# Weight quantization inside an attention and feed-forward kernel: half-width tiles with four load and two store buffers

## The reference

```python
def _weight_quant(w):
    scale = 1.0 / jnp.clip(jnp.mean(jnp.abs(w)), 1e-05)
    wq = jnp.clip(jnp.round(w * scale), -1.0, 1.0) / scale
    return w + jax.lax.stop_gradient(wq - w)

gate = jax.nn.silu(_bitlinear(x, w_gate))
up = _bitlinear(x, w_up)
return _bitlinear(gate * up, w_down)
```

## Time and profile before

| what | value |
|---|---|
| median of 11 runs | 3708.01 us (3695.86 to 3712.17) |
| profiled execution, its own time | 3701.79 us |
| span of its slowest core (core 1) | 3700.2 us |
| spans of the 8 cores | 3681.3 to 3700.2 us |
| TensorE (matmul), VectorE, ScalarE busy | 47%, 37%, 30% of the span |
| mean granted clock of the cores | 0.635 to 0.709 |

### The profile page before, as it was taken

One profiled execution on the slowest core, in us unless ns is written; L12 is line 12 of the kernel. 1 busy time (PEld: TensorE's weight loads), 2 busy tenths in 40 slices (PEclk: granted clock), 3 DMA queues, 4 the chain that ended last, 5 costly groups with the idle time before them and its releaser, 6 DMA issues.

```text
span 3700.2 us, 31906 instructions; the slowest of 8 cores (3681.3 to 3700.2 us)
## 1 busy us (share of the span) xinstructions
PE 1753.8 (47%) x8824; PEld 593.5 (16%) x8824; DVE 1354.7 (37%) x2709; ACT 1114.6 (30%) x1276; POOL 18.8 (1%) x55
## 2 busy tenths in 40 slices
PE   1211112222004443447477577728755862962874
PEld 0000000000001110111111111103322321421331
DVE  1442454444225554432321311134524524443352
ACT  1322322221120001547478488811201211220120
POOL 1000000000000000000000000000000000000000
PEclk9999998555555555555555555558987995986998
DMA  5445354222330000010100100023223322422522
GB/s 119 148 159 170 136 209 115 74 68 59 117 128 14 12 0 12 1 46 1 46 1 1 46 1 1 1 98 112 76 80 123 97 77 91 139 60 69 165 61 77
DMA packets 140978, 278.36 MB, mean 75 GB/s; under 512 B 7944, under 2 KB 106504, under 8 KB 134664
## 3 DMA queue, kind: packets, MB, share of 16 engines
q1 hardware_dynamic: 107256, 192.96, 15.8%
q10 hardware_dynamic: 24320, 67.12, 5.4%
q0 software_dynamic: 9232, 16.25, 2.8%
HBM read 250.61 MB, written 41.94 MB: 79 GB/s over the span
## 4 chain that ended last, share of the span: by engine, by line
PE 20%; ACT 15%; DVE 11%; DMA 7%; issue 5%; DVEq 1%; ACTq 0%; SPq 0%
PE ps_f L1076 6%; PE ps_f L1082 6%; PE ps_f L1190 5%; DMA wdbuf<-scr_d 4%; ACT PTb L747 4%; ACT PTb L743 4%; ACT PT L743 3%; ACT PT L747 3%; DMA xo_t<-xo 2%; ACT hqT L30 2%; DVE den_sb L821 1%; PE ps_sc L719 1%; DMA x1f<-scr_x 1%; PE ps_den L774 1%; DMA wubuf<-scr_u 1%
## 5 line engine op out<-in xcount | busy, mean ns | idle before, releaser
L719 PE MATMUL ps_sc<-qn,khat 32*128 32x512 bf16 (+3 forms) x1280 | 312.0, 529 | 136.8 <-ACT PT L743 50.1
L1190 PE MATMUL ps_f<-wdbuf,hqT 128*128 128x512 bf16 x1024 | 265.9, 410 | 99.8 <-DMA wdbuf<-scr_d 48.8
L1076 PE MATMUL ps_f<-wgbuf,xqT 128*128 128x512 bf16 x1024 | 248.3, 386 | 113.8 <-DMA wubuf<-scr_u 112.9
L1082 PE MATMUL ps_f<-wubuf,xqT 128*128 128x512 bf16 x1024 | 242.8, 380 | 0.0
L755 DVE TENSOR_TENSOR PT<-PT,maskD 128x512 bf16<-128x512 bf16 x64 | 27.2, 425 | 487.5 <-ACT PT L747 487.5
L323 ACT ACTIVATE wfbuf<-wfbuf,magicc,sclw 128x1024 f32<-128x1024 f32 (+1 forms) x48 | 100.5, 2093 | 322.9 <-DMA wfbuf<-wdT 173.1
L743 ACT ACTIVATE PT<-ps_sc,negMb 128x1024 bf16<-128x1024 f32 (+3 forms) x160 | 157.8, 986 | 121.3 <-PE ps_sc L719 109.1
L366 PE MATMUL ps_tr<-ident,xst 128*128 128x128 bf16 x384 | 52.2, 304 | 299.2 <-DVE xTc L29 207.4
L1096 DVE SCALAR_TENSOR_TENSOR hbuf<-ps_f,xsc,gate_s 128x512 f32<-128x512 f32 x128 | 96.1, 751 | 266.1 <-ACT gate_s L1090 266.1
L1090 ACT ACTIVATE gate_s<-ps_f,xsc 128x512 f32<-128x512 f32 x128 | 87.9, 687 | 345.0 <-PE ps_f L1082 345.0
L288 ACT ACTIVATE wqbuf_s<-wfbuf 128x1024 bf16<-128x1024 f32 (+1 forms) x48 | 91.7, 1910 | 276.0 <-DVE absacc L292 123.6
(11 more groups left out here) (224 smaller groups left out, 2366.8 us busy)
## 6 DMA issues: line engine op xcount, KB each, us to landing
wgbuf<-scr_g SPq DMA_DIRECT2D x32, 1024.0 KB, 6.3
wubuf<-scr_u SPq DMA_DIRECT2D x32, 1024.0 KB, 9.2
wfbuf<-wgT SPq DMA_DIRECT2D x8, 2048.0 KB, 9.7
wfbuf<-wgT ACTq DMA_DIRECT2D x8, 2048.0 KB, 8.9
wfbuf<-wuT SPq DMA_DIRECT2D x8, 2048.0 KB, 9.7
wfbuf<-wuT ACTq DMA_DIRECT2D x8, 2048.0 KB, 8.2
wfbuf<-wdT SPq DMA_DIRECT2D x32, 512.0 KB, 4.0
wfbuf<-wdT ACTq DMA_DIRECT2D x32, 512.0 KB, 4.0
```

The source lines that it names most:

```text
L719: e.matmul(ps_sc[:, j * 512 + stc:j * 512 + 512], khat[32 * j:32 * j + 32, gi * T + sc * 128: gi * T + sc * 128 + 128], qn[32 * j:32 * j + 32,
L1076: P.emit(t, lambda e, c=c, i4=i4, bi=bi, gb=gb: e.matmul(ps_f[:, gb:gb + 512], xqT[:, i4 * D + c * 128:i4 * D + c * 128 + 128], wgbuf[bi][ ...
L1082: P.emit(t, lambda e, c=c, i4=i4, bi=bi, ub=ub: e.matmul(ps_f[:, ub:ub + 512], xqT[:, i4 * D + c * 128:i4 * D + c * 128 + 128], wubuf[bi][ ...
L1190: e.matmul(ps_f[:, ((2 + i4) % 4) * 512: ((2 + i4) % 4) * 512 + 512], hqT[:, i4 * INNER + io * 128: i4 * INNER + io * 128 + 128], wdbuf[bi ...
```

## The change

The tiles of all three weights are halved in width: 16 tiles of 128 x 2048 for gate and for up, 64 tiles of 128 x 512 for down, two next to each other for each block of 128 rows. The two load buffers become four of half the size (`wf4`), used in turn, with four semaphores; the one store buffer becomes two of half the size (`wq4`). The SBUF space stays the same. Loads of even tiles still come from SP and those of odd tiles from ScalarE. A load of the first pass now waits for the magnitude instruction that read its buffer four tiles earlier, and no longer for a VectorE add or a store; a load of the second pass waits for the clip of four tiles earlier in place of two. A store buffer is awaited by the tile after next. `f0_step` and the places that call it are unchanged, and so is the order in which a step emits its instructions.

```diff
-                wfbuf = [b1("wfbuf0", [128, INNER], F32),
-                         b1("wfbuf1", [128, INNER], F32)]
-                wqbuf_s = b1("wqbuf_s", [128, INNER], BF16)
-                wqbuf = [wqbuf_s, wqbuf_s]
+                wf4 = [b1("wf4_0", [128, INNER // 2], F32),
+                       b1("wf4_1", [128, INNER // 2], F32),
+                       b1("wf4_2", [128, INNER // 2], F32),
+                       b1("wf4_3", [128, INNER // 2], F32)]
+                wq4 = [b1("wq4_0", [128, INNER // 2], BF16),
+                       b1("wq4_1", [128, INNER // 2], BF16)]
...
                         for wi, (src, dst, nt, ncols) in enumerate(
-                                [(dwg, sg, 8, INNER), (dwu, su, 8, INNER), (dwd, sd, 32, D)]
-                                if STAGE >= 1 else []):
+                                [(dwg, sg, 16, INNER // 2), (dwu, su, 16, INNER // 2),
+                                 (dwd, sd, 64, D // 2)] if STAGE >= 1 else []):
                             mk_z = P.emit(g, lambda e: e.memset(absacc[:], 0.0),
                                           waits=[(cV, cV.v)], incs=[(cG, 1)])
-                            vmk = [None, None]
+                            amk = [None, None, None, None]
+                            vmk_last = None
...
                             for i in range(nt):
-                                bi = i % 2
-                                w = [(cG, mk_z[1])] if i < 2 else []
-                                if dmk[bi] is not None:
-                                    w.append((qP[bi], dmk[bi][1]))
-                                if vmk[bi] is not None:
-                                    w.append((cV, vmk[bi][1]))
-                                mkd = P.emit(y if bi == 0 else "scalar",
-                                             lambda e, i=i, bi=bi, src=src, ncols=ncols:
-                                             e.dma_start(out=wfbuf[bi][:, 0:ncols],
-                                                         in_=src[i * 128:(i + 1) * 128, :]),
+                                bi = i % 4
+                                s2 = i % 2
+                                r = i // 2
+                                h = i % 2
+                                w = [(cG, mk_z[1])] if i < 4 else []
+                                if amk[bi] is not None:
+                                    w.append((cA, amk[bi][1]))
+                                elif vmq_carry[bi] is not None:
+                                    w.append(vmq_carry[bi])
+                                mkd = P.emit(y if bi % 2 == 0 else "scalar",
+                                             lambda e, r=r, h=h, bi=bi, src=src,
+                                             ncols=ncols:
+                                             e.dma_start(
+                                                 out=wf4[bi][:, 0:ncols],
+                                                 in_=src[r * 128:(r + 1) * 128,
+                                                         h * ncols:(h + 1) * ncols]),
                                              waits=w, incs=[(qF[bi], 16)], dma=True)
...
-                                wsm += [(qP[k], dmk[k][1]) for k in range(2) if dmk[k]]
-                                if vmk[0] is not None:
-                                    wsm.append(vmk[0])
-                                if vmk[1] is not None:
-                                    wsm.append(vmk[1])
-                                mka = P.emit(s, lambda e, bi=bi, ncols=ncols: e.activation(
-                                    wqbuf[bi][:, 0:ncols], wfbuf[bi][:, 0:ncols], AF.Abs,
-                                    accum_out=sm[:, 0:1]), waits=wsm,
-                                    incs=[(cA, 1)])
-                                vmk[bi] = P.emit(v, lambda e: e.tensor_add(
+                                if dmk[s2] is not None:
+                                    wsm.append((qP[s2], dmk[s2][1]))
+                                if vmk_last is not None:
+                                    wsm.append(vmk_last)
+                                mka = P.emit(s, lambda e, bi=bi, s2=s2, ncols=ncols:
+                                             e.activation(
+                                                 wq4[s2][:, 0:ncols],
+                                                 wf4[bi][:, 0:ncols], AF.Abs,
+                                                 accum_out=sm[:, 0:1]), waits=wsm,
+                                             incs=[(cA, 1)])
+                                amk[bi] = mka
+                                vmk = P.emit(v, lambda e: e.tensor_add(
                                     absacc[:], absacc[:], sm[:, 0:1]),
                                     waits=[(cA, mka[1])], incs=[(cV, 1)])
+                                vmk_last = (cV, vmk[1])
...
-                            vmq2 = [None, None]
+                            vmq2 = [None, None, None, None]
                             for i in range(nt):
-                                bi = i % 2
+                                bi = i % 4
+                                s2 = i % 2
+                                r = i // 2
+                                h = i % 2
                                 w = [(cV, mksc[1])]
                                 if vmq2[bi] is not None:
                                     w.append(vmq2[bi])
-                                elif dmk[bi] is not None:
-                                    w.append((qP[bi], dmk[bi][1]))
-                                mkd = P.emit(y if bi == 0 else "scalar",
-                                             lambda e, i=i, bi=bi, src=src, ncols=ncols:
-                                             e.dma_start(out=wfbuf[bi][:, 0:ncols],
-                                                         in_=src[i * 128:(i + 1) * 128, :]),
+                                elif amk[bi] is not None:
+                                    w.append((cA, amk[bi][1]))
...
-                                wv2 = [(qP[k], dmk[k][1]) for k in range(2) if dmk[k]]
-                                vmq = P.emit(v, lambda e, bi=bi, ncols=ncols: e.tensor_scalar_max(
-                                    wqbuf[bi][:, 0:ncols], wfbuf[bi][:, 0:ncols], -1.0),
-                                    waits=wv2, incs=[(cV, 1)])
+                                wv2 = ([(qP[s2], dmk[s2][1])]
+                                       if dmk[s2] is not None else [])
+                                vmq = P.emit(v, lambda e, bi=bi, s2=s2, ncols=ncols:
+                                             e.tensor_scalar_max(
+                                                 wq4[s2][:, 0:ncols],
+                                                 wf4[bi][:, 0:ncols], -1.0),
+                                             waits=wv2, incs=[(cV, 1)])
                                 vmq2[bi] = (cV, vmq[1])
-                                dmk[bi] = P.emit(y, lambda e, i=i, bi=bi, dst=dst, ncols=ncols:
-                                                 e.dma_start(out=dst[i * 128:(i + 1) * 128, :],
-                                                             in_=wqbuf[bi][:, 0:ncols]),
-                                                 waits=[(cV, vmq[1])], incs=[(qP[bi], 16)])
+                                dmk[s2] = P.emit(y, lambda e, r=r, h=h, s2=s2, dst=dst,
+                                                 ncols=ncols:
+                                                 e.dma_start(
+                                                     out=dst[r * 128:(r + 1) * 128,
+                                                             h * ncols:(h + 1) * ncols],
+                                                     in_=wq4[s2][:, 0:ncols]),
+                                                 waits=[(cV, vmq[1])],
+                                                 incs=[(qP[s2], 16)])
                                 yield
+                            vmq_carry = vmq2
```

More of the change, by code:

```diff
@@ L147, in build_nc @@
         qSm = mksem("qSm"); qW = mksem("qW"); qWo = mksem("qWo")
-        qF = [mksem("qF0"), mksem("qF1")]
+        qF = [mksem("qF0"), mksem("qF1"), mksem("qF2"), mksem("qF3")]
         qP = [mksem("qP0"), mksem("qP1")]
@@ L263, in f0_emitter @@
                         dmk = [None, None]
+                        vmq_carry = [None, None, None, None]
                         for wi, (src, dst, nt, ncols) in enumerate(
-                                [(dwg, sg, 8, INNER), (dwu, su, 8, INNER), (dwd, sd, 32, D)]
-                                if STAGE >= 1 else []):
+                                [(dwg, sg, 16, INNER // 2), (dwu, su, 16, INNER // 2),
+                                 (dwd, sd, 64, D // 2)] if STAGE >= 1 else []):
                             mk_z = P.emit(g, lambda e: e.memset(absacc[:], 0.0),
@@ L323, in f0_emitter @@
                                               e.activation(
```

(18 more changed lines are left out.)

## The result

The changed kernel took 3884.19 us (median of 8 runs, 3881.93 to 3892.6) against 3707.83 (31 runs): a ratio of 1.0481, 95% interval 1.0468 to 1.0493. The forecast was 3880 us, a slowdown. The profiled span grew from 3700.2 to 3880.4 us, by 180.2.

What follows compares the result with a forecast made beforehand. The drain was taken as bound by landings, not bytes or an engine: 260 us more there less 88 saved in the loop gives 172, so 3701.8 becomes 3874, or 3880 as a median; 8-in-10 range 3800 to 3960.

Steps and rivals of the forecast that it cites:

- the drain: Stretch between chunk loop and query stage where the emitter's remaining steps run, TensorE idle: 431 us against 171.5, 260 more.
- a fixed number of steps: Chunk loop: one emitter step behind each chunk's kvT copy, two behind each of four head steps, 72 before and after.
- Quantizing pairs: Second pass over down after the loop: two tiles with both landings waited for, 9.25 us each, 32 pairs, 296 us.
- magnitude pairs: First pass over down after the loop: two tiles with one landing waited for, 4.6 us each, 29 pairs, 133 us.
- the bounds of 2.1 and 4.0: Limits in us for a 256 KB landing after the loop: 2.1 gives -84 us, 4.0 gives +93.
- ScalarE's waits: ScalarE's waits for wdT landings after the loop: near 280 us, up from 141.
- the two slower rivals: Alternatives still slower than the kernel before: 256 KB landings near 2.1 us (3796), or no loop saving (3968); 12 in 100 each.
- even first: Loop head steps whose quantizing pair starts with the even tile: both landings inside the chain, 20.9 us each, 7 steps.
- odd first: Loop head steps starting with an odd quantizing tile: the even load waits for its VectorE passes, 29.6 us, 6 steps.
- Short landings: Rival, after the loop: 256 KB loads land like the store, near 2.1 us, giving 3796 us; 12 in 100.
- The loop saves nothing: Rival, chunk loop: landings stretch so it still ends at 939 us, giving 3968 us; 12 in 100.
- Deeper buffering hides the drain: Rival, after the loop: loads go out early enough that landings vanish, 152 us there, kernel 3600 us; 4 in 100.

Runs made afterwards that it cites:

- The wide tiles: Changed kernel with down's tiles back at 128 x 1,024 (32 tiles, 512 KB loads), gate, up and buffers as changed: 3745.7 us, ratio 1.0117.
- all loads ahead: Changed kernel with SP's and ScalarE's second-pass loads both issued two tiles earlier: 3658.5 us, ratio 0.9884 against the kernel before.
- the double steps: Changed kernel with the emitter called for twice as many steps in the chunk loop: 3943.4 us, ratio 1.0665 against the kernel before.
- The early memset: Changed kernel with the next weight's absacc memset emitted right behind the scale of the weight before: 3867.3 us, ratio 1.0454 against the kernel before.

## Why the prediction was right

*What bounds it.* The step that decided was to read the drain as a row of landings and the loop as a fixed number of steps. The wide tiles (the drain 142 us shorter with half the landings at equal bytes) and all loads ahead (the second pass of the drain 165 us shorter with equal tiles) show the first. Of the second, the double steps show that it isn't the number of steps as such: a step is only hidden if its landing lies under the chain.

*The drain.* Forecast 431 us, measured 418.6. The landing of 256 KB was taken as 3.0 and came out at 2.9 to 3.1. Quantizing pairs took 9.0 us against 9.25, magnitude pairs 4.4 against 4.6 (29 pairs in 128.5 us). With 93 landings counted and 93 found, the bounds of 2.1 and 4.0 were much wider than needed. ScalarE's waits were put near 280 us and came to 308: 93 landings of 3.0 are 279, and the time ahead of an even tile's issue counts as waiting too.

By the fit of the Trainium skill ("DMA: Bandwidth & Descriptors", Anatomy of one DMA), which is for GpSimd's path, the estimate for 256 KB was 2.6 us. The rows for SP and ScalarE say 2.9 to 3.1, so the trace lies 0.3 to 0.5 us above the fit.

*The loop.* Forecast was an end at 851 us and 88 us saved; measured 873.9 and 65. This is the term that was mis-sized, by 23 us. The drain's 12 us and the 2 us of the later stages make up for part of it, and the profiled run came out 8 us above its forecast; that the median came within 4 is in part luck. The range, too, held less than was said of it: the two slower rivals' own times, 3796 and 3968, lie just outside 3800 to 3960. The head steps came out as worked out: 18.4 us for magnitude (18.3), 20.9 to 21.3 for even first (20.9), 29.9 to 30.6 for odd first (29.6). One of the 32 was put down wrongly, the one with down's first tiles, at 17.05:

```profile
810.62 0.69 DVE L454 CAST krbuf<-ps_a 128x512 bf16<-128x512 f32 x1
...
826.05 0.42 DVE L532 COPY vtok<-ps_vt 128x512 bf16<-128x512 bf16 x1 [0.90 <-PE ps_vt L528]
...
826.66 0.10 POOL L270 MEMSET absacc<- 128x1 f32 x1 [269.38 <-DVE vtok L532]
...
826.89 4.57 SPq L287 DMA_DIRECT2D wf<-wdT  x3
...
827.17 1.48 POOL L548 DMA_DIRECT2D xst<-xo  x2 [0.41 <-issue]
...
830.49 0.33 ACTq L287 DMA_DIRECT2D wf<-wdT  x1
...
839.74 0.63 ACT L298 ACTIVATE wq<-wf 128x512 bf16<-128x512 f32 x1 [8.69 <-DMA wf<-wdT]
...
840.89 0.69 DVE L454 CAST krbuf<-ps_b 128x512 bf16<-128x512 f32 x1
```

It took 840.89 - 810.62 = 30.3 us. The memset is emitted in the step of down's first tile, hence behind the whole head step, and waits for its `vtok` copy. I had let it wait only for the last quantizing pass, a head step earlier. So SP's load goes out at 826.89, and ScalarE's, issued at 830.49, takes 9.2 us to its ACTIVATE; two x loads of the query stage left GpSimd's queue at 827.17. The early memset took 13 us off this step. The other 10 of the 23 are mostly spread over the other head steps, in pieces of under 2 us each; no run takes them apart.

*The rivals.* Short landings: no, 2.9 to 3.1. The loop saves nothing: no, 65 us. Deeper buffering hides the drain: not in this order of emission; with the loads ahead, in part: the drain falls to 254 us, where this rival had 152. Its condition was named rightly, the place in the queues. As the run with two load buffers shows, the double-buffering rule of the Trainium skill ("Trainium Kernel Development and Optimization", Best Practices) gave nothing in this case while that condition was not met.

## What to carry to other kernels

Count the landings that an engine waits for in full, and ask of each what stands ahead of its issue in that queue. More buffers did nothing here for a load that is issued behind the store or the ACTIVATE of the tile before; issue it two tiles earlier first, then size tiles and buffers. Where side work is handed out in a fixed number of steps, halving a step's size moves work to wherever the rest is drained, and the number of steps behind one chain should be no more than the landings that the chain hides.

## What the runs showed that was not expected

The same 64 tiles, in the same sizes and from the same queues, moved at 204 GB/s in one order of emission and needed 2.3 times as long in the other (288.5 us to 124). And one 256 KB load, where 2.9 us are usual, was followed by its ACTIVATE only after 9.2; two x loads had been issued from GpSimd's queue 3.3 us ahead of it. This was no single event: on all eight cores of that execution the same load took 8.1 to 10.2 us to its ACTIVATE, with the x loads 2.8 to 3.5 us ahead of it. That they held it up was not tried by itself.
